# Order of work in a fused two-layer attention kernel: group mean one tile later, half an output tile before the projection, two swaps on VectorE

## The reference

```python
# layer A: heads of 32 channels, windows of 32 tokens (one row of the image)
x = x + L0(gn(x))      # qkv = x @ w_qkv; softmax(q k^T / sqrt(32)) v in each window and head; @ w_proj + b_proj
# layer B: one head over all 1024 tokens of an image
x = x + L1(gn(x))      # energy[i, j] = k_i . q_j (32 channels); softmax over j; out = attn @ v; gamma * out

def gn(v, G=32, eps=1e-05):
    g = v.reshape(B, H, W, G, C // G)
    m = mean(g, axis=(1, 2, 4)); s = var(g, axis=(1, 2, 4))
    return ((g - m) / sqrt(s + eps)).reshape(v.shape)
```

## Time and profile before

| what | value |
|---|---|
| median of 3 runs | 668.62 us |
| runs | 664.68 to 669.41 us |
| the profiled execution | 666.09 us, of which the profile's span is 664.3 us |
| TensorE (PE) busy | 592.8 us, 89% of the span |
| VectorE (DVE) busy | 467.3 us, 70% |
| ScalarE (ACT) busy | 348.4 us, 52% |
| GpSimd (POOL) busy | 198.7 us, 30% |
| granted TensorE clock, mean | 0.969 |

### The profile page before, as it was taken

The page is one execution under the profiler, slowest core; times in us unless marked ns, Lnnn a source line. Parts: engine busy times, 40 slices in busy tenths (PEclk is TensorE's granted clock), DMA queues, the critical chain, the costliest instruction groups (busy, mean ns, idle before and its releaser), DMA issues.

```text
span 664.3 us, 15166 instructions
## 1 busy us (share of the span) xinstructions
PE 592.8 (89%) x5859; PEld 428.8 (65%) x5859; DVE 467.3 (70%) x765; ACT 348.4 (52%) x486; POOL 198.7 (30%) x198
## 2 busy tenths in 40 slices
PE   2888855899999999999999999999999999876887
PEld 2465732457785777568776778577766767654656
DVE  4565477587867787788868787878868875754562
ACT  2664243485268644874278535865387414631462
POOL 7423322302351315320450335231442142002203
PEclk9999977799999999999999999999999999887989
DMA  6122422133224313223223313331322232201001
GB/s 204 32 58 69 125 64 62 44 78 97 71 67 111 95 27 97 81 60 108 59 75 87 95 44 91 99 87 44 97 72 57 53 81 65 52 1 58 33 0 64
DMA packets 40116, 47.53 MB, mean 72 GB/s; under 512 B 6848, under 2 KB 32064, under 8 KB 40064
## 3 DMA queue, kind: packets, MB, share of 16 engines
q1 hardware_dynamic: 35312, 41.57, 23.8%
q10 hardware_dynamic: 4624, 4.98, 2.3%
q0 software_dynamic: 128, 0.26, 0.1%
HBM read 10.09 MB, written 8.39 MB: 28 GB/s over the span
## 4 chain that ended last, share of the span: by engine, by line
PE 70%; DVE 14%; ACT 5%; issue 4%; DMA 3%; SPq 2%; ACTq 0%; POOL 0%; POOLq 0%; DVEq 0%
PE pb L296 10%; PE pb L298 9%; PE pb L297 9%; PE pa L296 6%; PE pa L297 6%; PE pa L298 6%; PE pa L576 5%; PE pb L630 4%; PE pb L648 4%; DVE max_neg L1110 3%; PE pa L543 3%; PE pb L462 2%; PE pa L462 2%; DVE bst L1005 2%; ACT e L896 1%
## 5 line engine op out<-in xcount | busy, mean ns | idle before, releaser
L296 PE MATMUL pb<-v_h,e_h 128*128 128x257 f16 x448 | 123.9, 277 | 0.0
L298 PE MATMUL pb<-v_h,e_l 128*128 128x257 f16 x448 | 122.8, 274 | 0.0
L297 PE MATMUL pb<-v_l,e_h 128*128 128x257 f16 x448 | 122.5, 273 | 0.0
L1110 DVE TENSOR_REDUCE max_neg<-pb 128x1 f32<-128x1024 f32 x64 | 77.8, 1218 | 57.8 <-PE pb L630 57.6
L1125 DVE TENSOR_TENSOR e_l<-e,e_h 128x1024 f16<-128x1024 f32 x64 | 77.9, 1224 | 19.8 <-ACT e L896 18.4
L905 ACT ACTIVATE qk_h<-pb,y_fac 128x256 f32<-128x256 f32 x56 | 26.5, 472 | 108.8 <-DVE y_fac L1132 108.4
L896 ACT ACTIVATE e<-pb,f_energy 128x1024 f32<-128x1024 f32 x64 | 71.3, 1113 | 17.0 <-PE pb L648 17.0
L1331 POOL TENSOR_TENSOR y<-qk_h,y 128x256 f32<-128x256 f32 x64 | 45.9, 724 | 104.6 <-ACT qk_h L905 104.5
L1312 POOL TENSOR_TENSOR xb<-xin,bias 128x2048 f32<-128x2048 f32 x8 | 36.3, 4532 | 120.2 <-DVE x L1090 119.5
L1317 POOL TENSOR_TENSOR before_turn<-before_turn,a_rinv 128x1024 f32<-128x1024 f32 x16 | 30.6, 1915 | 113.3 <-DVE a_rinv L1071 107.9
L630 PE MATMUL pb<-q_stack,k_stack 96*128 96x512 f16 x128 | 40.6, 400 | 17.7 <-DVE max_neg L1110 8.2
(11 more groups left out here) (153 smaller groups left out, 1373.8 us busy)
## 6 DMA issues: line engine op xcount, KB each, us to landing
diag<-qkT SPq DMA_DIRECT2D x64, 128.0 KB, 2.4
xin<-in_x SPq DMA_DIRECT2D x15, 512.0 KB, 4.8
diag<-turned SPq DMA_DIRECT2D x60, 128.0 KB, 2.4
turned<-before_turn SPq DMA_DIRECT2D x118, 64.0 KB, 2.0
out<-y SPq DMA_DIRECT2D x24, 256.0 KB, 2.2
out<-y ACTq DMA_DIRECT2D x8, 256.0 KB, 2.1
q_stack<-qk_hl SPq DMA_DIRECT2D x8, 128.0 KB, 2.3
k_stack<-qk_hl SPq DMA_DIRECT2D x7, 128.0 KB, 2.4
```

Source lines behind the costliest of these rows:

```text
L296: nc.tensor.matmul(out_ap, lh, rh, start=start, stop=False)
L297: nc.tensor.matmul(out_ap, lh, rl, start=False, stop=False)
L298: return nc.tensor.matmul(out_ap, ll, rh, start=False, stop=stop)
L1110: nc.vector.tensor_reduce(max_neg[:, it:it + 1], energy_banks(b, it).rearrange("p a n -> p (a n)"), X, ALU.max, negate=True).then_inc(b_ma ...
```

## The change

On TensorE, where image i+2 exists, the group mean of norm "b" moves from behind tile 0 of the values' projection to behind tile 1, and the variance from ahead of tile 2 to ahead of tile 3. The first half (key tiles 0 to 3) of output tile 0 of image i moves from the start of `first(i + 1)` to the end of `second(i)`, ahead of the queries' projection, with a wait until VectorE has read the variance out of PSUM, since the tile uses the bank of the mean. On VectorE the maximum of energy 2 goes ahead of the transpose of the probabilities, and the low parts of queries and keys go between the row maximum and the subtraction of the first half of the scores.

```diff
@@ TensorE, first(i)
-                    if o and b and not next_to_last(i - 1): b_output(i - 1, it, b, range(0, 4))
+                    if o and b and not next_to_last(i - 1) and it > 0: b_output(i - 1, it, b, range(0, 4))
@@ TensorE, second(i)
-                    if m and j == 2: group_var("b", i + 1)
+                    if m and j == (3 if f else 2): group_var("b", i + 1)
                     if f: a_project_v(i + 2, (j,))
-                    if m and j == 0: group_mean("b", i + 1)
+                    if m and j == (1 if f else 0): group_mean("b", i + 1)
...
                 if f: a_scores(i + 2)
+                if b and f:
+
+                    pe.wait_ge(n_["b"]["ve"], nth(i + 1, 1, 1))
+                    b_output(i, 0, f, range(0, 4))
                 for c in range(CHUNKS):
                     if m: b_project_qk(i + 1, f, c)
@@ VectorE, first(i)
+                if b: b_maximum(i, 2)
                 if m: a_transpose(i + 1, 0)
-                if b: b_maximum(i, 2)
                 if f: stats("a", i + 2, (0,))
@@ VectorE, second(i)
                 if m: b_norm_split(i + 1)
-                if f: a_maximum(i + 2, 0)
+                if f: a_row_max(i + 2, 0)
                 if m: b_qk_low(i + 1)
+                if f: a_subtract(i + 2, 0)
```

## The result

| what | before | changed |
|---|---|---|
| median of 20 runs | 664.5 us | 666.9 us |
| runs | 663.04 to 669.41 us | 665.51 to 671.65 us |
| the profiled execution, its span | 666.09 us, 664.3 us | 665.92 us, 664.1 us |
| TensorE busy | 592.8 us | 589.2 us |
| granted TensorE clock, mean | 0.969 | 0.965 |

The ratio of the changed kernel to the one before is 1.0037, with a 95% interval of 1.0021 to 1.0053: slower by 2.4 us, which is under the 1% of the chances but clear of no change. With 20 runs the kernel before has a median of 664.5 us; the 668.62 us of the front page came from 3 runs.

What follows compares the result with a forecast made beforehand. TensorE's list was taken as the bound. Three slow and two fast steps plus 0 for the sixth gave +0.6 us, 666.1 to 666.7 us profiled; the median was put at 668.5 us, range 663.0 to 672.5 us.

Steps and rivals of the forecast that it cites:

- the 1% of the chances: Whole kernel: chance 0.11 of faster by over 1%, 0.06 of slower by over 1%, 0.83 of the same.
- the wait for the subtraction: Ahead of the input's transposes: TensorE waits 1.18 us for VectorE's second subtraction, in five steps.
- the sum: All six steps: three slow and two fast landings, 3 x 0.38 - 2 x 0.25 = +0.6 us, sixth boundary 0.
- TensorE's 0.80 us: Group mean of norm "b": moved a tile later, it no longer idles for VectorE's statistics, gaining TensorE 0.80 us.
- +0.38 and -0.25: Second half of layer A's output: change per step in us, with a slow and a fast landing of the spread's DMAs.
- the sixth boundary: Last step, without input transposes: TensorE's gain flows into energy 0's stack DMA wait; counted 0, between -0.6 and +0.4 us.
- energy 3 and the first transpose: Layer B's energies: energy 3 stops waiting and starts 0.56 us earlier; the first transpose of probabilities starts 1.5 us later.
- TensorE's place at the output of layer A: First half of layer A's output: TensorE arrives 0.3 us early, at 256.4 instead of 256.70.
- a slow landing: Second half of layer A's output: with long DMA landings the wait moves with the second transpose, +0.38 us a step.
- The rival of the clock: Behind the new wait at the input's transposes: clock falls to half, five times, 8.9 us in all, 677.5 us; chance 0.02.
- All idle time goes: Group mean and energy 3: both waits vanish and none replaces them, -10.4 us, 658.1 us; chance 0.10.
- The spread as the bound: First half of layer A's output: late spread of probabilities delays TensorE 1.2 us, six times 7.2 us, 675.8 us; chance 0.04.

Runs made afterwards that it cites:

- C: Edit: VectorE's maximum of energy 2 ahead of the first transpose of probabilities; as the only edit to the kernel before, 665.2 us, ratio 0.9987.
- D: Edit: low parts of queries and keys ahead of the scores' first subtraction on VectorE; as the only edit to the kernel before, 664.89 us, ratio 1.0006.
- C alone: Kernel before with only maximum 2 moved ahead of the first transpose of probabilities: 665.2 us, ratio 0.9987.
- A and C: Kernel before with group mean and variance a tile later and maximum 2 ahead of the first transpose of probabilities: 664.9 us, ratio 0.9996.
- A: Edit: group mean and variance of norm "b" a tile later on TensorE; as the only edit to the kernel before, 663.91 us, ratio 0.9980.
- A, B and C: Changed kernel with the first subtraction put back ahead of the low parts: 663.06 us, ratio 0.9974 to the kernel before.
- B: Edit: half an output tile ahead of the queries' projection on TensorE; not run as the only edit; with A 663.62 us, ratio 0.9970 to the kernel before.
- the second transpose first: A, B and C, plus VectorE's second transpose of probabilities ahead of norm "a"'s second statistics, its mean and variance later: 663.35 us, ratio 0.9968 to the kernel before.
- D alone: Kernel before with only the low parts moved ahead of the first subtraction: 664.89 us, ratio 1.0006.
- the one with the second row maximum: Changed kernel plus a second, unused row maximum on VectorE between low parts and first subtraction: 679.49 us, ratio 1.0213 to the kernel before.
- the version without C: Changed kernel with the first transpose of probabilities back ahead of maximum 2: 670.85 us, ratio 1.0065 to the kernel before.

## Why the prediction was right and wrong

The forecast was no change, by a sum of +0.6 us. In the profile the six steps grew by 6.1 us, and the medians differ by 2.4 us. The rows bear out the wait for the subtraction, in place and size. The step that failed is the sum. It took it that TensorE's 0.80 us arrive in each of five steps, that only the spread's landing decides between +0.38 and -0.25, and that the sixth boundary is worth 0. The runs show other things late: TensorE is held at the scores in steps one and three (2.5 us over the sum), step six has a half clock (1.84 us where 0 stood), and the output of layer A costs 1.2 us more than the sum gave it.

That 668.5 us lies only 1.6 us from the measured 666.9 is luck: the forecast started from a median of 668.62, which is 4.1 us too high, and this made up for the missed loss. From 664.5 the same sum gives 665.1 us.

**Right: the group mean, and the new wait.** The mean runs without idle time. The new wait was put at 1.18 us and is 240.94 - 239.64 - 0.11 = 1.19 us, in exactly five steps. The transposes start 0.27 us later than before in steps two and four, where I had 0.38. The overlap of neighbours on VectorE, on which this rests, is in the rows again (237.27 + 1.22 = 238.49 against a start at 238.41); to wait for an empty pipeline would have made it longer.

**Right in direction: energy 3 and the first transpose.** Energy 3 doesn't wait and starts at 33.22, 0.60 us earlier than before (I had 0.56). The first transpose of probabilities starts at 32.88 against 31.41 in step two, 1.47 us later (I had 1.5).

**Wrong: TensorE's place at the output of layer A.** I had TensorE 0.3 us early there. It comes 0.08 us late (38.97 against 38.89 and 38.88). I followed the maxima and the group mean on VectorE's list, but not `b_factor`, the two small instructions behind maximum 3, which release ScalarE's scaling of output tile 3. Output half 5 goes into that tile's bank. The rows of step two show it: energy 4's second matmul starts at 253.16, the output at 253.71, and a 512-column matmul is followed after 0.22 us, so 0.33 us are idle. The four other versions with C and without D (C alone; A and C; A, B and C; the second transpose first) have this wait in five steps; those without C have it once at most. So in the quiet step four the step is +0.11 us, where I had -0.3 to -0.22.

**Mis-sized: the second half of the output.** I gave a slow landing +0.38 us. In step two the second half comes at 45.23, 0.62 us later than before. The second transpose is 0.32 us late (38.20 against 37.88 from the anchor), the rest is the landing: for the four DMAs from 256.0 on it is

```profile
DMA to landing us min/median/max: 2.2/2.4/3.7
```

where the earlier trace rows have 3.4 at most for that spread. From 257 to 262 us and a step later, from 330 to 335 us, the queues of the DMA engines (packets, MB, share) are

```profile
q1 hardware_dynamic: 464, 0.79, 62.5%
q8 instruction: 1, 0.02, 1.5%
q14 instruction: 1, 0.01, 0.6%
```

```profile
q1 hardware_dynamic: 423, 0.76, 60.0%
```

and in the second stretch there is no wait. So the slow landings go with packets of instructions on the same engines. All spreads of steps one to six in the twelve profiles say the same: where no such packet ran between issue and landing, none landed later than 2.5 us; where one did, the slowest landed after 2.4 to 4.1 us (3.9 in step five of the changed kernel). That the one causes the other is likely and was not tried.

**Wrong: what TensorE wins at the group mean is not worth 0.80 us in every step.** In step one and in step three another thing is late at the scores, and I had looked at one boundary only. Timeline of TensorE, steps one and three, and the DMA queues from 303 to 307 us:

```profile
155.15 1.08 PE L543 MATMUL pa<-diag,qkT 128*32 128x128 f32 x32 [0.82 <-DMA diag<-qkT]
...
306.13 0.42 PE L543 MATMUL pa<-diag,qkT 128*32 128x128 f32 x5 [0.98 <-issue]
306.48 0.28 PE L296 MATMUL pb<-v_h,e_h 128*128 128x257 f16 x1
```

```profile
q1 hardware_dynamic: 289, 0.28, 19.8%
q8 instruction: 1, 0.02, 1.5%
```

In step one the scores wait for the spread of the keys; they start at 12.64, as before (12.66), and not 0.9 us earlier as in the other steps (11.75). In step three the last scores are held by nothing that the profile shows ("issue"), behind a packet of instructions. That stall ends at 16.4 from the anchor in both kernels. The kernel before reached it 0.9 us later and had little to lose there: its transposes start at 24.63 in step three, against 24.20 in step two. In the changed one it is 25.84 against 24.47. In step four, where the same code runs again, no packet of instructions and no stall are there.

The other profiles bear this out. The three versions without A lose 0.03 us at most there. Of the nine profiles with A eight have it in step three, and three in step two as well. In each of these eleven cases it ends 2.2 to 2.4 us after the start of a packet of 16384 bytes on an instruction queue, which starts at 13.7 to 14.2 from the anchor; in the profiles with A where the packet of these steps started at 13.1 or earlier, there is no stall. So a part of what A wins is lost again in the first steps, with D or without. The Trainium skill ("Runtime: NRT & Kernel Launch", Instruction fetch mechanics) has the crossing of such a block of instructions as mostly hidden. By that the stall would cost little; the row has 0.98 us. That the stall is the supply of instructions is my reading of these rows; no run isolated it. Steps one and three together are 2.5 us over my sum.

**Wrong: step six.** I counted 0, between -0.6 and +0.4 us. It is +1.84 us, the largest single miss. Timeline of TensorE, and two stretches as in the earlier trace rows:

```profile
534.02 0.60 PE L630 MATMUL pb<-q_stack,k_stack 96*128 96x512 f16 x2 [1.47 <-DMA k_stack<-qk_hl]
535.11 0.27 PE L296 MATMUL pb<-v_h,e_h 128*128 128x257 f16 x1 [0.48 <-ACT qk_h L909]
```

```profile
532.00:535.40 3.40, 1.45 (x10) 0.65 (x9) 3.30 (x7) 1.63 (x3) 0.02 (x1) 1.00 0.30 72
535.60:538.90 3.30, 3.30 (x15) 2.04 (x14) 2.20 (x4) 0.48 (x1) 2.37 (x2) 0.50 0.00 0
```

The wait for the stack's DMA grew from 0.5 to 1.47 us, as I had said (TensorE's gain flows into it). A wait of 0.48 us for ScalarE follows at once, TensorE is busy for 1.45 of 3.40 us, and then the clock is at 0.50 for 3.3 us, which costs some 1.65 us (half of it, with TensorE busy throughout). The rival of the clock, to which I had given 0.02 for the five new waits, did not come true there; it came true once, in the step for which I had not asked the question. The trace of before could have warned: a half clock lies in its step six too, from 569.2 on, behind 3.5 us in which TensorE was busy for 1.12. With A, B and C the stack's wait is 1.6 us too, but no second one follows: it is the wait for ScalarE that comes with D (it is also there with D alone, 0.5 us, once). The clock behind it, in the same form for TensorE alone, stays up:

```profile
532.30:535.60 3.30, 3.14 (x24) 1.00 0.00 0
```

The clock fell in three of the four profiles that have both waits (both of the changed kernel, and the one with the second row maximum), and in none of the other profiles. It held in the version without C, which has both. So the pair of waits brings the fall in most cases; what else decides is open.

**By steps**, sum against measurement: +0.38 and +1.60, +0.38 and +0.63, -0.25 and +1.01, -0.25 and +0.11, +0.38 and +0.93, 0 and +1.84 us. The missed 5.5 us are 2.5 from steps one and three, mostly the two stalls at the scores, 1.8 from step six, 0.55 in step five (a late second half again) and 0.6 from steps two and four.

**The rivals.** All idle time goes: not seen; the best versions gain 0.3%, not 10 us. The spread as the bound: in part, five waits of 3.2 us together in four steps, 2.5 of it at the second half; the place that the rival named, the first half, has 0.7. The chance for the same within 1% and the range of 663.0 to 672.5 us held the time; the sign of the change was not in the forecast.

## What to carry to other kernels

A wait taken from the busiest engine is worth only what the next late thing leaves, and that differs from step to step: go through every step of the trace, the first pass and the last one too, and not one typical boundary. Before an instruction that waits for another engine is moved ahead of independent work, look at what ran in that wait: here the first subtraction hid ScalarE's two high parts, and the swap cost 0.95 us a step once TensorE had become quicker. Where two edits give their gain to the same engine, measure them alone and together; the low parts' swap cost nothing alone and 0.6 to 1.1% with the others.

## What the runs showed of the hardware

- One idle stretch of 1.0 to 1.2 us of TensorE amid dense matmuls left the granted clock at 1.00 in five steps of five, in each of three profiles. One of 2.15 us put it to 0.50 for some 3.4 us in four steps of five. Waits of 1.5 us and of 0.5 us or more close together did so in step six in three profiles of four.
- TensorE stopped for 0.6 to 1.0 us in the middle of 128 small matmuls with nothing to wait for that the profile shows, in step three of eight profiles of nine with A and in step two of three. Each stop ended 2.2 to 2.4 us after the start of a packet of instructions, and none was in the second pass of the loop's code.
- DMAs of 128 KB landed after 2.2 to 2.5 us, and after up to 4.1 us where packets of instructions were moved in the same stretch.
